# Silu in place in PSUM, and the two halves of a step's gates set apart, in a graph attention kernel

## The reference, cut to what matters

```
dk = silu(edge_attr @ Wdk.T + bdk)        # edge_attr: 200000 x 64
dv = silu(edge_attr @ Wdv.T + bdv)        # both 256 wide: together the "gates"
attn = sum(q[dst] * k[src] * dk, axis=1)
attn = silu(attn) * cosine_cutoff(edge_weight)
msg  = v[src] * dv * attn[:, None]
agg  = segment_sum(msg, dst)              # 6250 x 256
out  = agg @ Wo.T + bo
```

## Time and profile before

| what | value |
|---|---|
| median of three executions | 2825.9 us |
| the profiled execution: its own time | 2828.56 us |
| its span, first to last instruction | 2826.3 us |
| PE busy | 2354.1 us (83%) |
| PEld busy | 1904.9 us (67%) |
| DVE busy | 2156.4 us (76%) |
| ACT busy | 1938.9 us (69%) |
| POOL busy | 2136.9 us (76%) |
| mean granted TensorE clock | 0.949 of full |
| HBM traffic | 227 GB/s over the span |

### The profile page before, as it was taken

How to read it: one execution, slowest core, us unless ns; L and a number is a source line. 1 busy time by engine, 2 the same in 40 slices (tenths; PEclk the granted TensorE clock), 3 DMA queues, 4 the chain that set the end, 5 groups by cost and what they waited for, 6 DMA issues and landing times. The chain is left out here.

```text
span 2826.3 us, 52157 instructions
## 1 busy us (share of the span) xinstructions
PE 2354.1 (83%) x12012; PEld 1904.9 (67%) x12012; DVE 2156.4 (76%) x6159; ACT 1938.9 (69%) x4051; POOL 2136.9 (76%) x1792
## 2 busy tenths in 40 slices
PE   7497888888888888888888888888888888888878
PEld 5254676676777676767676776766777767766666
DVE  4586878777878777787777787777777777777776
ACT  3474777777777677777777776777777777767766
POOL 1675878778787788777878778888877778777862
PEclk9799899999999999999999999999999999999999
DMA  8786777877888777788778778778877777778765
GB/s 237 198 215 242 211 234 229 238 234 227 235 236 230 228 224 227 226 234 237 227 231 232 228 234 237 233 229 232 234 231 229 233 231 229 224 234 233 223 188 182
DMA packets 321332, 642.50 MB, mean 227 GB/s; under 512 B 83932, under 2 KB 141648, under 8 KB 321304
## 3 DMA queue, kind: packets, MB, share of 16 engines
q0 software_dynamic: 129840, 418.60, 52.3%
q1 hardware_dynamic: 191464, 223.60, 25.7%
HBM read 583.26 MB, written 58.74 MB: 227 GB/s over the span
## 5 line engine op out<-in xcount | busy, mean ns | idle before, releaser
L949 POOL DMA_INDIRECT e_kv<-kv_tab,e_idx x1568 | 1959.3, 1250 | 495.4 <-issue 453.7
L1153 DVE TENSOR_TENSOR e_gated<-e_kv,e_gate 128x1024 f32<-128x1024 f32 x788 | 954.7, 1221 | 506.5 <-DMA e_kv<-kv_tab,e_idx 504.2
L1081 ACT ACTIVATE e_gate<-e_gate_ps 128x1024 f32<-128x1024 f32 x786 | 780.9, 1020 | 234.2 <-DVE e_gated L1153 217.1
L1097 ACT ACTIVATE weighed_hot<-hot,e_attn 128x128 f32<-128x128 bf16 x1580 | 520.4, 401 | 365.6 <-DVE e_attn L1172 353.9
L1000 PE MATMUL e_sum_ps<-e_gated,weighed_hot 128*128 128x256 f32 x3168 | 750.8, 380 | 3.9 <-ACT weighed_hot L1097 3.9
L1012 PE MATMUL e_gate_ps<-wd_hi_lo,high 128*128 128x512 f32 x1572 | 677.2, 431 | 13.5 <-issue 13.5
L1000 PEld LDWEIGHTS e_sum_ps<-e_gated,weighed_hot 128*128 128x128 f32 x3168 | 603.6, 191 | 101.2 <-ACT weighed_hot L1097 4.7
L1013 PE MATMUL e_gate_ps<-wd_bias,low 128*128 128x512 f32 x1572 | 650.3, 414 | 0.0
L1162 DVE CUSTOM_DVE_ANT_0 e_gated<-e_gated,e_q_ps 128x256 f32<-128x256 f32 x1576 | 573.9, 415 | 0.7 <-PE e_q_ps L1032 0.7
L1031 PE MATMUL e_q_ps<-q_win,hot_t 128*128 128x256 f32 x1572 | 465.1, 323 | 47.7 <-DVE e_dot L1162 47.4
L1020 PE MATMUL e_hot_ps<-ident_bf,hot 128*128 128x128 bf16 x1568 | 160.3, 226 | 315.6 <-DVE hot L1179 315.4
(11 more groups left out here) (156 smaller groups left out, 1398.7 us busy)
## 6 DMA issues: line engine op xcount, KB each, us to landing
e_attr<-attr_groups_dram SPq DMA_DIRECT2D x784, 128.0 KB, 4.6
e_q_next<-q_tab SPq DMA_DIRECT2D x98, 256.0 KB
e_kv<-kv_tab,e_idx POOLq DMA_INDIRECT x1568, 4.5
sum_tab<-e_sums SPq DMA_DIRECT2D x100, 128.0 KB, 4.3
e_prior<-sum_tab SPq DMA_DIRECT2D x99, 128.0 KB
kv_tab<-l_kv_out SPq DMA_DIRECT2D x49, 256.0 KB, 3.5
q_tab<-l_q_out SPq DMA_DIRECT2D x49, 256.0 KB, 3.2
sum_tab<-zeros SPq DMA_DIRECT2D x25, 256.0 KB, 2.9
```

The lines of the kernel that those rows point to most:

```text
L949: pool.indirect_dma_start(kv[:, k, :], None, kv_tab, bass.IndirectOffsetOnAxis(ap=idx[:, k:k + 1], axis=0)).then_inc(kv_landed[k // G][k % ...
L1081: nc.scalar.activation(gate[:, 2 * p:2 * p + 2, :], gate_ps[:, 2 * p:2 * p + 2, :], ACT.Silu).then_inc(silu_ready[s][p], 1)
L1097: last = nc.scalar.activation(weighed_hot[:, s % 2, k, :], hot[:, s, :, k], ACT.Copy, scale=attn[:, s * G + k:s * G + k + 1])
L1153: nc.vector.tensor_tensor(gated[:, pair(s, p), :], kv[:, pair(s, p), :], gate[:, 2 * p:2 * p + 2, :], ALU.mult).then_inc(gated_ready[s][p], 1)
```

## The change

The silu writes its result over its own input in `gate_ps`, and `gate_rows` multiplies from there; the buffer `gate` in SBUF is gone. A product into a half of `gate_ps` now waits for the `gate_rows` of that half (`gated_ready`), where it waited for the silu, and the silu no longer has a wait of its own for `gate_rows`. On PE, ACT and DVE the two halves no longer follow one another: PE has the sums, the turning and the first `gather_q` between them, ACT has `weigh`, DVE has the one-hots and the first dots. `attend` stands ahead of the second dots and of `low_attr`. The start-up copies of ACT write to `gate_ps`, and PE waits for them once.

```diff
--- before.py
+++ after.py
@@ -825,7 +825,6 @@
         q_next = sb("q_next", [P, 2 * H], F32)
         place = sb("place", [P, BLOCK_TILES], BF16)
         gated = sb("gated", [P, BLOCK_TILES, 2 * H], F32)
-        gate = sb("gate", [P, G, 2 * H], F32)
         dot = sb("dot", [P, BLOCK_TILES], F32)
         silu_dot = sb("silu_dot", [P, BLOCK_TILES], F32)
         cut_now = sb("cut_now", [P, BLOCK_TILES], F32)
@@ -1006,7 +1005,7 @@
                     s = slot(c, 1)
                     if p == 0:
                         pe.wait_ge(low_ready[s], visit.of(c, 1))
-                    pe.wait_ge(silu_ready[slot(c, 2)][p], visit.of(c, 2))
+                    pe.wait_ge(gated_ready[slot(c, 2)][p], visit.of(c, 2))
                     for k in (2 * p, 2 * p + 1):
                         cols = slice(k * P, (k + 1) * P)
                         nc.tensor.matmul(gate_ps[:, k, :], high[:, s % 2, cols], wd_hi_lo[:], start=True, stop=False)
@@ -1033,18 +1032,19 @@
                     last.then_inc(q_done[s][p], 1)
 
                 pe.wait_ge(dve_ready, 1)
+                pe.wait_ge(act_ready, 1)
                 with pe.Fori(0, all_visits(pe)):
                     for c in range(GROUPS):
+                        segment_sum(c, 0)
                         gates(c, 0)
-                        gates(c, 1)
-                        segment_sum(c, 0)
                         segment_sum(c, 1)
                         turn_hot(c)
+                        gather_q(c, 0, visit.of)
+                        gates(c, 1)
                         of = visit.of
                         if c == GROUPS - 1:
                             visit.step()
                             of = visit.of_last
-                        gather_q(c, 0, of)
                         gather_q(c, 1, of)
                 for c in range(GROUPS):
                     for p in range(2):
@@ -1076,9 +1076,8 @@
 
                 def silu(c, p):
                     s = slot(c, 1)
-                    act.wait_ge(gated_ready[slot(c, 2)][p], visit.of(c, 2))
                     act.wait_ge(gate_done[s][p], visit.of(c, 1))
-                    nc.scalar.activation(gate[:, 2 * p:2 * p + 2, :], gate_ps[:, 2 * p:2 * p + 2, :], ACT.Silu).then_inc(silu_ready[s][p], 1)
+                    nc.scalar.activation(gate_ps[:, 2 * p:2 * p + 2, :], gate_ps[:, 2 * p:2 * p + 2, :], ACT.Silu).then_inc(silu_ready[s][p], 1)
 
                 def take_window():
 
@@ -1104,7 +1103,7 @@
                     nc.scalar.copy(hot_t[:, c % 2, :, :], hot_ps[:, 0:G, :]).then_inc(hot_t_ready[c], 1)
 
                 for k in range(0, G, 2):
-                    last = nc.scalar.copy(gate[:, k:k + 2, :], weighed_hot[:].rearrange("p a k n -> p a (k n)"))
+                    last = nc.scalar.copy(gate_ps[:, k:k + 2, :], weighed_hot[:].rearrange("p a k n -> p a (k n)"))
                 last.then_inc(act_ready, 1)
                 nc.scalar.preload_act_table(ACT.Silu)
                 act.wait_ge(dve_ready, 1)
@@ -1115,8 +1114,8 @@
                             take_window()
                         round_attr(c)
                         silu(c, 0)
+                        weigh(c)
                         silu(c, 1)
-                        weigh(c)
                         copy_hot(c)
                     visit.step()
                 for c in range(GROUPS - 1):
@@ -1150,7 +1149,7 @@
                     s = slot(c, 2)
                     dve.wait_ge(kv_landed[s][p], visit.now32 if c >= 2 else visit.late32)
                     dve.wait_ge(silu_ready[s][p], visit.of(c, 2))
-                    nc.vector.tensor_tensor(gated[:, pair(s, p), :], kv[:, pair(s, p), :], gate[:, 2 * p:2 * p + 2, :],
+                    nc.vector.tensor_tensor(gated[:, pair(s, p), :], kv[:, pair(s, p), :], gate_ps[:, 2 * p:2 * p + 2, :],
                                             ALU.mult).then_inc(gated_ready[s][p], 1)
 
                 def dot_rows(c, p):
@@ -1201,7 +1200,6 @@
                         for c in range(GROUPS):
                             if c:
                                 gate_rows(c, 0)
-                            gate_rows(c, 1)
                             if c == 0:
                                 dve.wait_ge(hot_ready[GROUPS - 1], visit.prev)
                                 nc.vector.tensor_scalar(place[:], dst_f[:, bass.ds(t * BLOCK_TILES, BLOCK_TILES)], window_f[:, bass.ds(t, 1)],
@@ -1212,14 +1210,15 @@
                             else:
                                 one_hot(c)
                                 dot_rows(c, 0)
+                            gate_rows(c, 1)
+                            attend(c)
                             dot_rows(c, 1)
                             low_attr(c)
-                            attend(c)
+                            if c == GROUPS - 1:
+                                take_sums()
                             if c == 2:
                                 dve.wait_ge(attn_ready[GROUPS - 1], visit.prev)
                                 nc.vector.tensor_copy(cut_now[:], cut[:, bass.ds(t * BLOCK_TILES, BLOCK_TILES)]).then_inc(cut_ready, 1)
-                            if c == GROUPS - 1:
-                                take_sums()
                         visit.step()
                         gate_rows(0, 0)
                 for c in range(GROUPS - 1):
```

## The result

The changed kernel takes 2479.7 us (median of 4 executions, 2477.2 to 2488.3), the kernel before 2833.5 beside it: ratio 0.8755, 95% interval 0.8709 to 0.8801. The prediction was 2533 us, range 2440 to 2710. The profiled execution took 2488.3 us against 2828.6 before: 340 us less, where 294 were forecast.

A forecast was written before the change was run, and what follows sets the result against it. POOL's gather queue, held by `gate_rows`, was taken as the bound at 25.0 us a visit. POOL's 20.2 + 1.2 = 21.4 plus 0.6 gave 22.0; 3.0 x 98 = 294 us gained, so 2533 us, range 2440 to 2710.

The forecast's parts named there:

- Part 1: `gate_rows` reading gates from PSUM stops holding POOL's gathers: 4.6 us a visit gained (bounds 0 to 4.8), POOL's need 20.2.
- The check on the size: Eight `gate_rows` of 1.2 us, met by a gather every 1.25 us, cost 4.6 us a visit, against 4.8 excess.
- Part 2: ACT's silu written over its input in PSUM: taken as 0 change, bounds 0.1 less to twice as long.
- Part 3: Half of `gate_ps` held until `gate_rows` ends, 3.5 us against a 5.5 us step: 1.1 us slack, no cost.
- Rival C: POOL stays held and late `gate_rows` delay their half's matmuls, 3.3 us a visit at full, half taken: 2990 us, chance 0.09.
- Part 5: POOL waits for the other half's gathers to land: 0.6 us twice, 1.2 a visit (bounds 0.2 and 3.2).
- part 4: Earlier `attend` shrinks ACT's wait without end gain; later `gate_rows(c,1)` may make POOL wait 0 to 0.3 us.
- A: DMA queues fill, landing takes 6.3 us, POOL stands 1.6 us twice a visit: 2700 us, chance 0.16.
- the 0.6 us for four resources that never fit perfectly: Allowance added to the visit because POOL, PE, DMA and DVE needs lie within 8%: 0.6 us, giving 22.0.
- my 19.3 to 21.3: PE's time a visit in us: 19.3 at full clock, 21.3 now with 1.2 GHz stretches; denser work should recover some.

## Why the prediction was right

**The bound and its cause** were read rightly: POOL's queue was full, and its long gathers were holds by `gate_rows`. The run with PSUM alone and the table of holds show it. The signs named beforehand came too: no gather of the stretch over 1.5 us, DVE's wait for k and v under 2 us a visit, PE's two waits 1.4 us together.

**Part 1, the release.** 4.6 us a visit were forecast to go; the mean fell by 0.273 x 16 = 4.4. I counted the one-hots as what stays (0.2 us; 20.5/92.75 = 0.22 measured) and left out `low_attr`, another two-input instruction, 23.1/92.75 = 0.25. With the spacing POOL's need is 16 x 0.976 + 436.2/92.75 = 20.3 against 20.2. The check on the size, 4.6 us by gathers that meet the eight `gate_rows` at random, agreed with the measured 4.8 partly by luck: in the changed order with SBUF the same eight held 16 x 0.320 = 5.1 us, and all holds together 5.8. The forecast does not hang on it, since nearly all of the excess goes either way.

**Where page and trace seem to differ.** The Trainium skill ("SBUF — State Buffer", Who interferes with whom) infers that `tensor_tensor` leaves descriptor generation alone, and the prediction said that the trace decides against this. What the runs decide against is the conclusion that such a gather loses nothing: 356 us of holds before, 0.4 with one input in PSUM and the order left alone. The inference itself they leave standing. The same section says that a DVE instruction with two SBUF inputs contends with a GpSimd instruction that reads SBUF, and a gather reads its row numbers from the SBUF tile `idx`. In the trace only the gather's first part is held: a held gather takes 0.82 us more once it is let go, of 0.947 in all, so it stood some 0.13 us after its start. And 124 gathers of the kernel before met no two-input instruction at that point and a `gate_rows` that began 0.4 to 0.95 us after their start: none took over 0.95 us. That it is the row numbers that wait fits this, but no run shows it. The section's rule on one SBUF input holds here.

**Part 2, in place.** Silu 13 ns shorter, `gate_rows` 9 ns; nothing was the right cost.

**Part 3, the ring.** The slack was there on a usual chip, even in the order of before: DVE waited for the silu 14.8 us in 2000 with the changed order and 1.1 with that of before. Rival C did not come.

**Part 5, what is late next.** Landing waits 1.2 us forecast, 86.0/92.75 = 0.93 measured, with 0.23 for `gate_rows` (0 to 0.3 in part 4) and 0.1 for indices. A stayed small.

**The term of the sum that was mis-sized** is the 0.6 us for four resources that never fit perfectly. POOL's own terms, 20.3 + 1.2 + 0.1, already are the visit of 21.6; the others fit beside it. PE helped: 1865.28/92.75 = 20.1 us a visit, inside my 19.3 to 21.3, since the clock stayed at its upper level (1.00). 0.44 us x 98 = 43 us are the 46 between 294 and 340.

**What the prediction missed altogether** is that the gain depends on the chip. As a ratio, its range ended at 2710/2826 = 0.96; the other kind gave 1.02.

## What to carry to other kernels

Compare the median of POOL's gathers with their mean; where they differ, lay the long ones beside DVE's timeline, look for instructions with both inputs in SBUF, and move one input of the longest to PSUM. When a queue is full, add up its own terms, and be sparing with an allowance on top for the other engines: 0.6 us a visit was too much here. Time a change that makes transfers denser on more than one chip: here its sign changed.

## What the runs showed that I had not expected

- A held gather ends 0.82 us after the end of a two-input DVE instruction (526 of 526 in the kernel before). When such instructions run back to back it can be held over all of them, up to 3.63 us from start to end.
- Who comes first matters, and DVE can wait too, though briefly: 20 of the 788 `gate_rows` of the kernel before took 1242 to 1300 ns (the others at most 1240). Each time a gather had begun within 0.04 us of it, and took its free 0.94 to 0.95 us.
- Of the 49 gathers that began inside `take_sums` in 300 to 2300 us of the kernel before, 36 were held to the end of the `gate_rows` behind it, though `take_sums` has one input in PSUM and the `gate_rows` began only 0.25 us after the gather. What takes hold so early stays open.
- On two chips the kernel before took 14% longer, and the ranking was reversed: there the gates in SBUF with the changed order were best (0.965), and PSUM with the order of before worst (1.089).
